# Queries split four heads at a time, and a new order of work on VectorE and ScalarE

## The reference

```
x = x + einsum('bct,bcd->bdt', x, W0[cond])                    # layer 0
x = x + (x @ base_w.T + bias + lora(x, adapter ids))           # layer 1
q, k, v = x @ Wq.T, x @ Wk.T, x @ Wv.T                         # layer 2: 32 query heads, 8 key heads of 128
q, k = rope(rmsnorm(q)), rope(rmsnorm(k))
k_all = concat(k_cache[block_table], k); v_all = concat(v_cache[block_table], v)   # 512 + 32 tokens
probs = softmax(where(valid, q @ k_all.T / sqrt(128), -1e30))
x = x + (probs @ v_all) @ Wo.T
x = x + einsum('bct,bcd->bdt', x, W3[cond])                    # layer 3
```

## Time and profile before

| | |
|---|---|
| median of 3 runs | 2390.94 us (2390.47 to 2391.7) |
| the profiled execution | 2394.14 us |
| its span | 2392.4 us |
| granted TensorE clock, mean | 0.994 of full speed |
| busy: PE, DVE, ACT, POOL | 97%, 74%, 64%, 58% of the span |
| attention, first to last score matmul | 726.6 to 2173.2 us |

### The profile page before, as it was taken

The page is one execution under the profiler, slowest core; times in us unless marked ns, Lnnn a source line. Parts: engine busy times, 40 slices in busy tenths (PEclk is TensorE's granted clock), DMA queues, the critical chain, the costliest instruction groups (busy, mean ns, idle before and its releaser), DMA issues.

```text
span 2392.4 us, 58277 instructions
## 1 busy us (share of the span) xinstructions
PE 2312.0 (97%) x15392; PEld 2010.2 (84%) x15392; DVE 1760.8 (74%) x5422; ACT 1535.2 (64%) x4221; POOL 1395.5 (58%) x2249
## 2 busy tenths in 40 slices
PE   8999999999998899999999999999999999998999
PEld 5778888888887788888888888888888888887777
DVE  4434777777778887887887887887887887886232
ACT  4324666666667777777777777777777777775221
POOL 1003454444447777877877877877877877872000
PEclk9999999999998999999999999999999999999999
DMA  4335333333337777777767777777767777775332
GB/s 164 95 110 163 102 98 102 111 106 102 97 115 257 221 224 239 253 228 237 255 223 241 253 228 237 255 223 242 252 220 245 253 223 241 253 221 194 110 132 101
DMA packets 347959, 455.96 MB, mean 191 GB/s; under 512 B 34506, under 2 KB 280842, under 8 KB 343695
## 3 DMA queue, kind: packets, MB, share of 16 engines
q1 hardware_dynamic: 308398, 315.83, 41.9%
q0 software_dynamic: 36864, 134.23, 16.9%
q10 hardware_dynamic: 2528, 4.29, 0.5%
HBM read 374.53 MB, written 79.69 MB: 190 GB/s over the span
## 4 chain that ended last, share of the span: by engine, by line
PE 48%; DVE 23%; issue 19%; ACT 5%; POOL 3%; DMA 1%; DVEq 0%; ACTq 0%; POOLq 0%; SPq 0%
PE S L1168 11%; PE oP L1168 11%; DVE regC L987 8%; PE S L1260 7%; DVE k_lo L284 7%; PE oP L1241 3%; PE oP L1092 3%; DVE regC L986 3%; PE S L1209 3%; PE bank L1092 2%; PE oP L1122 2%; ACT regC L721 2%; PE bank L1260 2%; DVE nmx L975 1%; DVE rinv L981 1%
## 5 line engine op out<-in xcount | busy, mean ns | idle before, releaser
L1241 PE MATMUL oP<-regC,regK 128*128 128x128 f32 x4096 | 541.2, 275 | 0.1
L1241 PEld LDWEIGHTS oP<-regC,regK 128*128 128x128 f32 x4096 | 507.2, 192 | 9.6 <-issue 0.3
L975 DVE CUSTOM_DVE_ANT_0 regC<-S,mask 128x544 f32<-128x544 f32 x512 | 368.1, 719 | 187.9 <-issue 185.7
L715 ACT CAST k_hi<-regK 128x544 fp32r<-128x544 f32 x512 | 331.3, 647 | 210.5 <-PE S L1209 184.1
L721 ACT ACTIVATE regC<-regC,nmx 128x544 f32<-128x544 f32 x512 | 384.9, 752 | 58.8 <-DVE nmx L975 49.8
L534 POOL TENSOR_TENSOR regC<-regC 128x256 f32<-128x256 f32 x320 | 244.3, 784 | 278.3 <-DVE regC L944 278.3
L549 POOL TENSOR_TENSOR q_hi<-regC,ones 128x128 fp32r<-128x128 f32 x512 | 262.3, 512 | 233.8 <-PE S L1209 229.1
L1092 PE MATMUL bank<-ident,regC 128*128 128x128 f32 x2048 | 321.1, 279 | 26.9 <-ACT regC L765 21.0
L284 POOL TENSOR_TENSOR k_lo<-regK,k_hi 128x192 fp32r<-128x192 f32 x512 | 341.4, 667 | 3.3 <-ACT k_hi L715 3.3
L987 DVE TENSOR_SCALAR regC<-regC,rinv 128x512 f32<-128x512 f32 x512 | 337.8, 660 | 0.0
L284 DVE TENSOR_TENSOR k_lo<-regK,k_hi 128x352 fp32r<-128x352 f32 x512 | 328.2, 641 | 2.9 <-ACT k_hi L715 2.9
(11 more groups left out here) (137 smaller groups left out, 4468.9 us busy)
## 6 DMA issues: line engine op xcount, KB each, us to landing
regK<-kT_cache SPq DMA_DIRECT2D x1024, 128.0 KB
qkT_d<-regC SPq DMA_DIRECT2D x160, 256.0 KB, 2.3
regC<-qkT_d SPq DMA_DIRECT2D x64, 512.0 KB
oT_d<-regC SPq DMA_DIRECT2D x64, 256.0 KB
regK<-oT_d SPq DMA_DIRECT2D x16, 1024.0 KB, 5.0
regC<-wqk SPq DMA_DIRECT2D x10, 1024.0 KB, 5.2
v_d<-regC SPq DMA_DIRECT2D x32, 256.0 KB, 2.3
regK<-qkT_d SPq DMA_DIRECT2D x64, 128.0 KB
```

The lines of the kernel that those rows point to most:

```text
L715: nc.scalar.copy(k_hi[u % 2].rearrange("p (s t) -> p s t", t=PSIZE), k_sb[b][:, :, h, :]).then_inc(s_khi, 1)
L975: nc.vector.tensor_tensor_reduce(out=p_sb[u % 4], in0=scores, in1=mask[u // HK % 2][:], scale=-SCALE, scalar=3e38, op0=ALU.add, op1=ALU.mi ...
L1241: last = nc.tensor.matmul(oP[:, j * 512:j * 512 + P], v_sb[b][:, m, u % HK * D:(u % HK + 1) * D], pT_sb[u % 2][:, m * P:(m + 1) * P], star ...
```

## The change

POOL keeps the gathers and the index copies, and loses `split_q` and its share of `k_lo`. ACT makes `q_hi` with a copy and DVE `q_lo` with a subtraction, for four heads at once (512 columns, HW), in two buffers each. DVE makes the whole of `k_lo` (544 columns). `score` takes its head's 128 columns of the four. The steps of DVE, ACT and PE have a new order: DVE splits k for head n+3 (was n+4) and does so first; ACT's exponential is that of head n+1 (was n+2) and stands first; PE transposes the own probabilities at the end of a step with u%4 of 3 instead of at the start of one with u%4 of 0, and turns p at the same place in each step. SP has a semaphore `s_q` of its own for the queries. Tiles are laid out anew, `ones` goes, and `ids` lies in another region.

```diff
-        KLOAD = 16 * (NPP + 2)
+        KLOAD = 16 * (NPP + 1)
@@ SP, group
-                        sp.wait_ge(s_qp, g * UG + HK * (k + 1))
-                        load_own(b, k % 2)
+                        sp.wait_ge(s_qp, g * (2 * BT) + 2 * (k + 1))
+                        load_q(b, k % 2)
                         sp.wait_ge(s_klo, g * UG + HK * (k + 1))
+                        load_own_k(b, k % 2)
                         load_pages(b, k % 2)
@@ POOL
-                nc.gpsimd.tensor_tensor(q_hi[u % 2], q, ones[:], ALU.mult).then_inc(s_qhi, 1)
-                pool.wait_ge(s_qhi, n + 1)
-                nc.gpsimd.tensor_tensor(q_lo[u % 2], q, q_hi[u % 2].bitcast(F32), ALU.subtract)
-                pool.wait_ge(s_khi, n + 1)
-                k_low(nc.gpsimd, b, h, u, slice(LOW, NPP + 1)).then_inc(s_qp, 1)
...
-                if not (fixed and n + 4 >= NU):
-                    split_q(n + 4, u + 4, g * 2 + (u + 4) // (2 * HK))
@@ ACT
+            def split_q(m, u, pair):
+                b, h = u // HK % 2, u % HK
+                if h == 0:
+                    act.wait_ge(s_q[b], pair * 16 + 16)
+                ge(act, s_qk, m * 4 - 4)
+                nc.scalar.copy(q_hi[u // 4 % 2], q_sb[b][:, h * P:h * P + HW]).then_inc(s_qhi, 1)
...
                 if u % 4 == 0 and not (fixed and n == 0):
                     own_turned(g, u)
+                if not (fixed and n + 1 >= NU):
+                    exps(n + 1, u + 1)
                 if not (fixed and n + 4 >= NU):
                     split_k(n + 4, u + 4, g * 2 + (u + 4) // (2 * HK))
-                if u % 4 == 0:
-                    if not (fixed and n + 2 >= NU):
-                        exps(n + 2, u + 2)
-                    if not (fixed and n == 0):
-                        out_heads(g, u)
                 act.wait_ge(s_ta, n + 1)
                 ge(act, s_pv, n - 1)
                 nc.scalar.copy(pT_sb[u % 2], pT).then_inc(s_evA, 1)
-                if u % 4 and not (fixed and n + 2 >= NU):
-                    exps(n + 2, u + 2)
+                if u % 4 == 0 and not (fixed and n == 0):
+                    out_heads(g, u)
+                if u % 4 == 3 and not (fixed and n + 5 >= NU):
+                    split_q(g * (UG // 4) + (u // 4 + 2), u + 5, g * 2 + (u + 5) // (2 * HK))
@@ DVE
-                k_low(nc.vector, b, h, u, slice(0, LOW)).then_inc(s_klo, 1)
+                lo, hi = (k[u % 2].rearrange("p (s t) -> p s t", t=PSIZE) for k in (k_lo, k_hi))
+                nc.vector.tensor_tensor(lo, k_sb[b][:, :, h, :], hi.bitcast(F32), ALU.subtract).then_inc(s_klo, 1)
+            def split_q(m, u):
+                b, h, i = u // HK % 2, u % HK, u // 4 % 2
+                dve.wait_ge(s_qhi, m + 1)
+                nc.vector.tensor_tensor(q_lo[i], q_sb[b][:, h * P:h * P + HW], q_hi[i].bitcast(F32), ALU.subtract)\
+                    .then_inc(s_qp, 1)
...
-                if u % HK == 3 and not (fixed and n + HK >= NU):
-                    make_mask(g * BT + (u // HK + 1), (u // HK + 1) % 2)
-                if not (fixed and n + 1 >= NU):
-                    inverse(n + 1, u + 1)
+                if not (fixed and n + 3 >= NU):
+                    split_k(n + 3, u + 3)
                 if not (fixed and n + 2 >= NU):
                     masked_max(n + 2, u + 2, g * BT + (u + 2) // HK)
                 if not (fixed and n + 1 >= NU):
+                    inverse(n + 1, u + 1)
                     normalise(n + 1, u + 1)
-                if not (fixed and n + 4 >= NU):
-                    split_k(n + 4, u + 4)
+                if u % HK == 3 and not (fixed and n + HK >= NU):
+                    make_mask(g * BT + (u // HK + 1), (u // HK + 1) % 2)
+                if u % 4 == 1 and not (fixed and n + 3 >= NU):
+                    split_q(g * (UG // 4) + (u // 4 + 1), u + 3)
                 if u % HK == 4:
                     out_low(g, u // HK)
@@ PE
-            def score(n, u):
+            def score(n, u, m):
                 pe.wait_ge(s_klo, n + 1)
-                pe.wait_ge(s_qp, n + 1)
+                if u % 4 == 0:
+                    pe.wait_ge(s_qp, m + 1)
                 ge(pe, s_mx, n)
...
-                pe.wait_ge(s_evA, g * UG + u)
-                nc.tensor.transpose(pT[:, 0:P], po_sb[(u - 4) // 4 % 2], ident[:]).then_inc(s_tb, 1)
+                pe.wait_ge(s_evA, g * UG + u + 1)
+                nc.tensor.transpose(pT[:, 0:P], po_sb[u // 4 % 2], ident[:]).then_inc(s_tb, 1)
...
-                if u % 4 == 0 and not (fixed and n == 0):
-                    turn_own(g, u)
                 if not (fixed and n + 2 >= NU):
-                    score(n + 2, u + 2)
-
-                if u % 4:
-                    turn_p(g, u)
+                    score(n + 2, u + 2, g * (UG // 4) + (u + 2) // 4)
+                turn_p(g, u)
...
-                if u % 4 == 0:
-                    turn_p(g, u)
+                if u % 4 == 3:
+                    turn_own(g, u)
```

More of the change, by code:

```diff
@@ L175, in build @@
         oT_hi = parts("oT_hi", H2 * P)
-        q_hi, q_lo = [parts("q_hi0", P)], [parts("q_lo0", P)]
-        k_hi, k_lo = zip(*([parts(f"{name}{i}", KW) for name in ("k_hi", "k_lo")] for i in range(2)))
-        o_st = inC(T)
-        x2r = inC(T)
+        q_hi, q_lo = [parts("q_hi0", HW)], [parts("q_lo0", HW)]
+        k_hi = [parts("k_hi0", KW)]
         po_sb = [inC(P) for _ in range(2)]
+        assert at[0] <= 12 * T
+        at[0] = 12 * T
+        k_lo = [None, parts("k_lo1", KW)]
+        k_hi.append(parts("k_hi1", KW))
+        q_hi.append(parts("q_hi1", HW))
+        q_lo.append(parts("q_lo1", HW))
         p_next = [inC(KW) for _ in range(3)]
@@ L184, in build @@
         pTo_sb = inC(P)
+        o_st = inC(T)
+        x2r = inC(T)
         oT_lo = parts("oT_lo", H2 * P)
-        at[0] = 27 * T
+        assert at[0] <= CSZ - 2 * KW
+        at[0] = CSZ - 2 * KW
         p_sb = [inC(KW)] + p_next
-        q_hi.append(parts("q_hi1", P))
-        q_lo.append(parts("q_lo1", P))
+        k_lo[0] = parts("k_lo0", KW)
         o3_hi, o3_lo = ((y, x) for x, y in zip((oT_hi, oT_lo), o3_parts))
         xy = [o_st, x2r]
-        ones = sb("ones", [P, P])
         mask = [sb(f"mask{i}", [P, KW]) for i in range(2)]
@@ L259, in build @@
         s_k = [sem(f"s_k{i}") for i in range(2)]
+        s_q = [sem(f"s_q{i}") for i in range(2)]
         s_v = [sem(f"s_v{i}") for i in range(2)]
@@ L279, in tile @@
             return i + j // 4, j % 4, i * 4 + j
-        def k_low(engine, b, h, u, slots):
-            lo, hi = (k[u % 2].rearrange("p (s t) -> p s t", t=PSIZE)[:, slots, :] for k in (k_lo, k_hi))
-            return engine.tensor_tensor(lo, k_sb[b][:, slots, h, :], hi.bitcast(F32), ALU.subtract)
         @block.sync
@@ L289, in _ @@
             SP = [mybir.EngineType.SP]
-            for dst, src in ((cond[:], cond_row), (ids[:], id_row)):
+            for dst, src in ((cond[:], cond_row), (ids, id_row)):
                 sp.dma_start(dst, src).then_inc(s_ids, 16)
@@ L571, in _ @@
                 add_halves(QKB - 1, t)
-                if t in (NT - 4, NT - 2):
-                    u = (t - (NT - 4)) // 2
-                    split_q(u, u, 0)
-            for u in range(2, 4):
-                split_q(u, u, 0)
             for u in range(ROT):
@@ L1033, in _ @@
             split_k(1, 1)
-            for u in range(2):
-                masked_max(u, u, 0)
-                split_k(u + 2, u + 2)
+            masked_max(0, 0, 0)
+            split_k(2, 2)
+            masked_max(1, 1, 0)
             inverse(0, 0)
@@ L1198, in block_qk @@
                     if last and t == NT - LAG:
-                        score(0, 0)
-            def score(n, u):
+                        score(0, 0, 0)
+            def score(n, u, m):
                 pe.wait_ge(s_klo, n + 1)
-                pe.wait_ge(s_qp, n + 1)
+                if u % 4 == 0:
+                    pe.wait_ge(s_qp, m + 1)
                 ge(pe, s_mx, n)
+                head = slice(u % 4 * P, (u % 4 + 1) * P)
                 halves = (slice(0, 9 * PSIZE), slice(9 * PSIZE, KW))
-                for m, (q, k) in enumerate(((q_hi, k_hi), (q_hi, k_lo), (q_lo, k_hi))):
+                for i, (q, k) in enumerate(((q_hi, k_hi), (q_hi, k_lo), (q_lo, k_hi))):
                     for at in halves:
-                        last = nc.tensor.matmul(scores[:, at], q[u % 2], k[u % 2][:, at],
-                                                start=(m == 0), stop=(m == 2))
+                        last = nc.tensor.matmul(scores[:, at], q[u // 4 % 2][:, head], k[u % 2][:, at],
+                                                start=(i == 0), stop=(i == 2))
                 last.then_inc(s_qk, 1)
@@ L1300, in _ @@
             block_qk(QKB - 1, 1, True)
-            score(1, 1)
+            score(1, 1, 0)
             pe.wait_ge(s_qT, QKB * NT)
@@ L1312, in _ @@
                 step(NT - 1, u, None)
-            turn_own(NT - 1, UG)
             values(NT - 1, UG - 1)
```

37 lines of the change are left out of this document (17 added, 20 removed).

## The result

The changed kernel takes 2505.1 us (median of 4 runs, 2501.4 to 2506.6) against 2391.3 of the kernel before in the same session. The ratio is 1.0477, with an interval of 1.0465 to 1.0489: 114 us slower. The forecast was 2455 us with a range that ended at 2490; the direction was right, the size was not. The profiled execution took 2501.4 us, its span is 2499.6 us at a mean granted clock of 0.993 (before 2392.4 us, 0.994).

What follows compares the result with a forecast made beforehand. The prediction took TensorE to bound the kernel: a group goes from 90.0 to 94.5 us (68.1 + 26.4) through waits for `q_lo`, fifteen groups +67.5 us, the first -4, in sum +64, giving 2455 us. Range 2410 to 2490.

Steps and rivals of the forecast that it cites:

- The mechanism: In the attention, TensorE's score waits for VectorE's `q_lo` seven times a group, 1.1 or 2.1 us each.
- the long wait: At u = 5, 13, 21 and 29, `q_lo` comes late behind `out_low`: TensorE waits 2.1 us.
- the short one: At u = 9, 17 and 25, the next score starts at S + 3.20 instead of S + 2.08: 1.1 us.
- The step that failed: TensorE's steps without `out_proj`: eight without a wait take 18.1 us, the 25 of a group about 56.
- Before, about 6.5 us of the 62.65 are thus waits of TensorE: In the 25 steps without `out_proj`, the kernel before holds about 6.5 us of TensorE waits a group.
- The two lines of the view of waits: Waits before the change: POOL's part of `k_lo`, 11.9 us in 20; the copy of pT, 11.6 in 40.
- Rival 1: VectorE, rid of POOL, is in time and TensorE runs near its floor: about 2280 us, chance 0.13.
- The second term: The seven `out_proj` steps of a group lose 0.9 us of waits, from 27.35 to 26.4 us.
- The third: The first group, with `split_wo` in steps 8 to 23, changes by -4 us, between -8 and +4.
- Rival 2: `q_lo` is in time, only `out_low` delays the maximum, 0.8 us four times a group: 2388 to 2395 us, chance 0.07.
- If L986 stayed at its median: VectorE's 32-column scaling stays long, 0.19 us at seven waits; with L284 longer too, +32 us: 2487 us.

Runs made afterwards that it cites:

- f1: The changed kernel with each value gather held back until the score of its own step is done, one gather a step: 2501.4 us, ratio 1.0459.
- f2: The changed kernel with `q_lo` made one step earlier and the value gathers paced one a step: 2365.5 us, ratio 0.9889.
- e3: The changed kernel with `turn_own` at u = 11, 15, 19, 23 and 27 writing to an idle bank, without waiting for the copy: 2523.0 us, ratio 1.0568.
- f4: The changed kernel with `turn_own` at five places a group in an idle bank and the gathers paced: 2506.1 us, ratio 1.0473.
- g1: The changed kernel with `q_lo` early, `k_lo` ahead of `out_low`, `turn_own` in the idle bank at five places and paced gathers: 2340.4 us, ratio 0.9785.
- e4: The kernel before, in its order, with all 544 columns of `k_lo` on VectorE while GpSimd keeps the queries: 2363.9 us, ratio 0.9892.
- e7: The changed kernel with three unused subtractions of 96, 96 and 192 columns added on GpSimd in each step: 2548.0 us, ratio 1.0658.

## Why the prediction was right or wrong, point by point

**The mechanism was right.** The place of `q_lo` costs 136 us (f1 against f2), more than the whole loss of 114. The chain of the long wait came within 0.05 us at each link, the short one within 0.01: 3.20 us at u = 9, 17 and 25 (forecast 3.20), 4.13 at u = 5, 13, 21, 29 (forecast 4.18). `k_lo` took 718 ns (0.71 forecast), `q_lo` 684 (0.69), the small scaling 241 (0.23), and no wait for POOL was left. u%4 of 0 took 2.68, as 2.08 + 0.6.

**The step that failed** is "Eight steps without a wait are 8 x 2.08 + 2 x 0.6 + 2 x 0.11 = 18.1 us, and the 25 about 56", a floor that was too low, and with it "Before, about 6.5 us of the 62.65 are thus waits of TensorE". Measured, the eight steps of u = 14 to 21 take 21.75 us, of which (3.20 - 2.11) + (4.13 - 2.11) = 3.1 are waits for `q_lo`, the 3.2 of the forecast; the floor is 18.6. The missing 0.5 is the price of `turn_own`, a wait that the prediction put at nothing: I had costed it as one transpose, 0.11, and it costs 2.42 - 2.08 = 0.34 twice in eight steps, as it stands behind the values and waits for ACT's copy of pT, and the next score behind it. Moved to where it waits for nothing it costs the 0.11 (2.19 us, e3, f4 and g1). I had named where `turn_own` moves, but not the wait that it gets there. In addition u = 7 and u = 23 take 2.60 and 2.78 instead of 2.42. With the other bank u = 23 takes 2.20 as well, so its excess hung on the same wait (the loop ends there, ROT being 24); u = 7 kept its bank and its 2.60, and was not looked into. Together 3 x 0.45 + 0.18 + 0.36 = 1.9 us a group, the whole of 69.98 against 68.1, and in fifteen groups 28 of the 43 us that are missing.

By the same error the waits of before were too large: from f2 the floor of the 25 steps in the change's order is 61.5 - 4 x 0.78 = 58.4 us, so before had 4.3 us of waits to give back to it and not 6.5. (With `turn_own` in the other bank the floor is 57.0, by g1, and the waits are 5.7.) The two lines of the view of waits that it quotes had named 2.4 us of them a group; the other 4.1 were only the difference to the floor, and that was the place to doubt it. Rival 1 had been priced with the 6.5, at 2280.

**The second term** is "In the seven `out_proj` steps I count one of the first and one of the second, 0.9 us". Step by step only u = 1 got shorter, 3.75 to 3.51; u = 0 and 4 got 0.03 longer each. The part fell by 0.16 us, not 0.9, which makes 12 us in fifteen groups: the seven steps held 0.2 us of waits that the change takes away and not 0.9. That the matmuls of `out_proj` covered the others is likely but not shown.

**The third** is the first group, "I take -4 us, between -8 and +4". It takes 102.1 us against 98.8 (from the first score to the 33rd): +3.2. VectorE's shorter instructions are there, but `split_wo` adds to the chain ahead of `q_lo`: four steps of 3.06 to 3.81 us (u = 9, 13, 17, 21) became 4.70 to 4.78, while those of u = 11 and 19 fell from 3.81 to 2.33. And the waits of u = 5 and 29, outside `split_wo`, came here as in any group, 1.6 us each.

**The sum** then closes: the attention starts 1.0 us earlier, the first group adds 3.2, the fourteen full groups 99.2 (1260.5 to 1359.7), the last 5.6: 107.0 of the span's 107.2. The forecast had 67.5 for the last fifteen where 104.8 stand, and -4 for the first: 43.5 us, all of the 43 between 2458 and the profiled 2501.4. The range missed it as its bounds came from durations and chains alone, and none from the floor, which counted fifteen times over.

**The rivals.** Rival 1 (VectorE in time) fell for this kernel, though its argument that VectorE has something to win was sound: in e4, where `q_lo` isn't VectorE's, the lighter GpSimd gives 26 us. Rival 2 (`q_lo` in time, `out_low` holding back the maximum by 0.8 us four times a group) is what f2 is, 0.77 us each: its price was right. It had added that VectorE's 18.7 us against 18.1 cost 0.6 to 1.5 more in eight steps; against TensorE's real 18.6 they cost nothing, all other steps of f2 being at their floor. Its sum was loose as well: 56.3 + 26.4 + 3.2 and three times 0.6 to 1.5 is 87.7 to 90.4 us a group, and it took the upper end for its 2388 to 2395. f2 takes 88.67, so what had been forecast as no change is 26 us faster. The bound "If L986 stayed at its median" didn't come true. How it spread the price didn't hold either: it put 0.2 us or so on each of seven waits, 32 us in all; in e7, with the median at 348, the steps of u = 9, 17 and 25 lost 0.8 us each, u = 1 lost 0.5, and the four long waits nothing, 43 us in all.

## What to carry to other kernels

In an engine that runs its list in order, price a moved item from the moment at which its reader needs it and along all that stands ahead of it; sums of work, busy shares and idle time say nothing on that, and moving one line by one step was worth 136 us here. Read the floor of a step where nothing waits, for each kind of step apart, and treat an instruction that starts just after another engine's end as one that waited, even if the view doesn't name it: what repeats fifteen times over thirty-two steps has to be right to the tenth. When a repair that should work changes nothing, look for where the time came back before giving up the theory; here late signals around bursts of gathers hid it, and pacing the gathers brought it out.
